# Where the expert matmuls stand in a block's window: ahead of or behind the next projection

## The reference

```python
x = layernorm(x + attn(x))         # conv (3 taps, 1024 -> 768), 16 heads in blocks of 128,
                                   # then o @ proj_w + proj_b, (256 -> 1024)
base = x @ W_base.T + b_base       # 1024 -> 1024
gate = softmax(x @ W_gate.T)       # 8 experts
thr = sigmoid(x @ W_thr.T + b_thr) / 8
w = max(gate - thr, 0); w = w / (sum(w) or 1)
h = x @ A.T                        # 8 experts of rank 16 -> 128 columns
moe = (h * w) @ B * 2              # 128 -> 1024
x = layernorm(x + base + moe)
```

## Time and profile before

| | us |
|---|---|
| median of 3 runs | 1800.07 (1799.27 to 1800.44) |
| the profiled execution's own time | 1800.44 |
| its span | 1798.6 |
| of the span, PE busy | 1743.6 (97%) |
| DVE busy | 1438.9 (80%) |
| ACT busy | 723.2 (40%) |
| POOL busy | 333.0 (19%) |

### The profile page before, as it was taken

One profiled execution on the slowest core, in us unless ns is written; L12 is line 12 of the kernel. 1 busy time (PEld: TensorE's weight loads), 2 busy tenths in 40 slices (PEclk: granted clock), 3 DMA queues, 4 the chain that ended last, 5 costly groups with the idle time before them and its releaser, 6 DMA issues. The chain is left out here.

```text
span 1798.6 us, 32713 instructions
## 1 busy us (share of the span) xinstructions
PE 1743.6 (97%) x11712; PEld 1599.5 (89%) x11712; DVE 1438.9 (80%) x3281; ACT 723.2 (40%) x1881; POOL 333.0 (19%) x276
## 2 busy tenths in 40 slices
PE   5899999999999799999999999999999999999998
PEld 5899999899999688888888888878898989898987
DVE  8977679977767688888888888887878787878785
ACT  4332334333324576767777767771111111111110
POOL 6100003400000110100101001134333333333331
PEclk9999999999999899999999999999999999999999
DMA  4323223432342101010110101223121212121211
GB/s 139 114 76 99 82 76 110 149 88 82 94 169 88 54 1 48 1 47 0 47 47 0 47 0 63 85 82 105 54 79 53 77 54 77 54 75 56 75 42 48
DMA packets 48804, 123.03 MB, mean 68 GB/s; under 512 B 5488, under 2 KB 13680, under 8 KB 48240
## 3 DMA queue, kind: packets, MB, share of 16 engines
q1 hardware_dynamic: 48752, 122.36, 20.6%
HBM read 88.79 MB, written 33.55 MB: 68 GB/s over the span
## 5 line engine op out<-in xcount | busy, mean ns | idle before, releaser
L388 PE MATMUL conv_acc<-x_split,weights 128*128 128x256 f32 x4608 | 555.2, 283 | 32.3 <-DVE weights L314 25.0
L388 PEld LDWEIGHTS conv_acc<-x_split,weights 128*128 128x128 f32 x4608 | 552.4, 190 | 34.9 <-DVE weights L314 26.5
L1343 PE MATMUL ps_f<-weights 128*128 128x266 f32 (+2 forms) x1728 | 329.0, 343 | 0.0
L1343 PEld LDWEIGHTS ps_f<-weights 128*128 128x128 f32 x1728 | 277.4, 189 | 23.5
L247 ACT ACTIVATE x_split<-x_mixed 128x1024 fp32r<-128x1024 f32 x128 | 135.7, 1060 | 305.7 <-PE conv_acc L388 276.7
L309 DVE TENSOR_TENSOR x_split<-x_mixed,x_split 128x1024 fp32r<-128x1024 f32 x128 | 158.3, 1237 | 99.9 <-ACT x_split L247 99.9
L720 ACT ACTIVATE scores_and_probs<-scores_and_probs,score_neg_max 128x128 f32<-128x128 f32 x512 | 197.9, 392 | 3.5 <-DVE score_neg_max L831 3.5
L1179 ACT ACTIVATE gate_exp<-h_and_gate,gate_neg_max 128x8 f32<-128x8 f32 x32 | 9.6, 301 | 347.1 <-DVE gate_neg_max L1254 347.1
L683 POOL TENSOR_TENSOR weights<-conv_tile,weights 128x1024 fp32r<-128x1024 f32 x14 | 36.1, 2576 | 476.0 <-ACT weights L703 384.6
L826 DVE CUSTOM_DVE_ANT_0 scores_and_probs<-ps_scores,causal_mask 128x128 f32<-128x128 f32 x512 | 117.8, 286 | 0.5
L1343 PE MATMUL ps_f<-q_k_pairs,weights 128*128 128x266 f32 (+2 forms) x576 | 117.0, 338 | 0.0
(11 more groups left out here) (118 smaller groups left out, 2651.7 us busy)
## 6 DMA issues: line engine op xcount, KB each, us to landing
x_raw<-in_xT SPq DMA_DIRECT2D x128, 257.0 KB, 2.7
conv_tile<-in_x SPq DMA_DIRECT2D x32, 512.0 KB, 3.4
out<-out_tile SPq DMA_DIRECT2D x32, 512.0 KB, 2.6
convT_scratch<-features_out SPq DMA_DIRECT2D x16, 768.0 KB, 3.5
conv_tile<-convT_scratch SPq DMA_DIRECT2D x16, 768.0 KB, 6.4
conv_w_raw<-in_conv_w SPq DMA_DIRECT2D x16, 576.0 KB, 3.9
weight_stage<-in_ffn_w SPq DMA_DIRECT2D x8, 581.0 KB, 3.7
yT_scratch<-features_out SPq DMA_DIRECT2D x8, 512.0 KB, 3.7
```

Source lines behind the costliest of these rows:

```text
L388: last = nc.tensor.matmul(acc[f][k // 2][:, k % 2, :], w[:, c, a, k, f * P:(f + 1) * P], xs[:, c % XS, b, k, :], start=(c == 0 and k % 2 = ...
L1343: mm = nc.tensor.matmul(ps_f[par][n][:, 0:b0 - a0], x1T[:, par, a, kc, :], wf[kc][:, b, a0:b0], start=(kc == 0 and k == 0), stop=(n == 2 a ...
```

## The change

In PE's window the call of `experts(i, par)` moves ahead of the call of `project(i + 2, par)`. No instruction is added, removed or changed.

```diff
                 base(i, par, 1, range(CC // 2, CC))
+                experts(i, par)
                 if not last(n, 2):
                     project(i + 2, par)
-                experts(i, par)
```

## The result

| kernel | median, us | range, us | runs |
|---|---|---|---|
| before | 1800.26 | 1799.27 to 1801.06 | 4 |
| after | 1813.99 | 1813.25 to 1815.96 | 4 |

The change makes the kernel slower: 13.7 us lie between the two medians. Three more executions of the kernel after took 1815.11, 1816.99 and 1817.49 us. The ratio of the means over all seven is 1.0084 (95% interval 1.0069 to 1.0098), which is 15.1 us. The forecast was 1813.8 us. The profiled execution of the kernel after has a span of 1813.9 us, 15.3 more than before's.

What follows compares the result with a forecast made beforehand. PE was taken to bound the last phase, with DVE not far behind. Lateness of 8.15 us plus restarts of 5.5 us gave 13.7 us, so 1813.8 us was predicted, range 1809 to 1820 us.

Steps and rivals of the forecast that it cites:

- DVE's chain: DVE's work from its second add of the projection to the end of L1282, 13.87 us, following project wherever it is put.
- The sum: Last phase: lateness 8.15 us plus restarts 5.5 us make 13.7 us, between 9.9 and 19.2.
- Window in the loop: Windows 4 to 27: experts 1.50, project's start to second add 2.96, chain 13.87, together 18.33 us, plus 0.19 restart.
- from project's start to the second add: Piece of the closed loop from PE's project start to DVE's add of the projection's second half, 2.96 us.
- the slack of windows 2, 3 and 28: Operand slack in windows outside the loop, taken as 1.31 us without being read; range widened to 1809 to 1820.
- The restart: PE resuming after each wait at the experts: 0.06 us wake-up plus 0.13 us first weight load, 29 times, 5.5 us.
- The high end: Restart in which PE's sequencer also loses its lead: 0.38 us a window, 11.0 us in all.
- A: Rival: DVE's normalising step takes 0.81 instead of 2.80 us, chain 11.88 us, PE never waits, 1800.1 us; 8%.
- B: Rival: restart costs far more than 0.38 us a window; at 0.6 us, 1825.6 us; 5%.
- C: Rival: short waits bring down PE's clock in the last phase, 1839 us; 4%.
- D: Rival: faster, because the experts' early end frees `ps_f` or smooths PE's order; 3%.

Runs made afterwards that it cites:

- e7: Kernel after with one 0.2 us instruction (L1268) left out of DVE's chain; median 1810.50 us, ratio to before 1.0043.
- e4: Kernel after with one more DVE instruction in the chain, L1246's split of y repeated into a spare tile; median 1826.83 us, ratio to before 1.0142.
- e5: Kernel before with one more DVE instruction, L1246's split of y repeated into a spare tile; median 1803.43 us, ratio to before 1.0011.
- e1: Kernel after with DVE's split_hT(i) put ahead of its split_xT(i + 1) in each window; median 1800.60 us, ratio to before 0.9993.
- e6: Kernel after with POOL's bias add (L1143) made on one column instead of 1024, from block 2 on; median 1800.38 us, ratio to before 0.9993.
- e8: Kernel before with six more DVE instructions in each window, L1246's split repeated into spare tiles; median 1829.91 us, ratio to before 1.0155.

## Why the prediction was right

*The spare time of the moved operand is not what the trace of before shows at its place.* The prediction read 1.20 us of slack and set 1.50 us of delay against it, because DVE's chain hangs on project. The trace after has the chain unchanged at 13.87 us and the wait where it was said, in 29 windows. e7 and e4 show that the chain enters the window one for one, e5 that it doesn't before.

*The sum.* Window in the loop: forecast 18.33 + 0.19 = 18.52, measured 18.51 in the turn shown above and up to 18.55 in others. From the first window to the last 14.3 us came on top, forecast 13.7. The excess is small and spread, 29 windows by 0.02 us. The piece that was too short is the one from project's start to the second add: forecast 2.96, measured 2.98 in 11 windows and 3.01 or 3.02 in 19. The 2.98 belong to the new order, for e1 has them without any wait (its second add starts at 1507.92, project at 1504.94). The rest shows in e4 and e7 too, where the experts wait for DVE, and not in e1 and e6, where they don't; what makes it was not looked for. That the medians lie 13.7 us apart, to the digit of the forecast, is luck: over all seven executions it is 15.1 us, and the time ahead of the phase varies by 1 us and more. The range was widened for the slack of windows 2, 3 and 28. That wasn't needed: their slots, too, open 1.3 us after the operand is ready.

*The restart.* The wake-up is 0.06 us as forecast; the experts' group is 1.77 us long behind the wait and 1.67 without, so the first load costs 0.10 where I took 0.13 from a group in the attention. Together 0.16 instead of 0.19, 0.9 us less over 29 windows, which hides a part of the excess above. The high end, in which the sequencer's lead is lost, did not show: after the wait project starts 1.60 us behind the experts, 1.50 + 0.10.

*The rivals.* A did not happen: POOL stayed 0.14 us ahead of DVE, the distance that hangs on POOL alone. Its chain of 11.88 us was 0.3 us too short, by e6; the time that it gives doesn't change by that. By the Trainium skill's rule (SBUF — State Buffer, "Who interferes with whom") the first to issue holds the shared ports and the other one blocks. That the two instructions disturb each other agrees with e6, where the short POOL instruction leaves DVE's at 0.81 us; that the order decides was not tested, for no run has it the other way round. The rule says that the second one blocks fully; here DVE's step of 0.81 us ends 0.55 us after POOL's, so by estimate 0.26 us of it ran beside POOL's. B did not happen, see the restart. C did not: the granted clock was 1.00 from 1222 to 1790 us. D, a gain from the order itself, shows in the traces but is tiny. Where the new order runs without waits, in e1 and e6, the first and last start of L1282 are closer together than before. Of e1:

```profile
L1282 DVE TENSOR_TENSOR h_weighted_T<-ps_f,h_weighted_T x32: 236/238/293, 1232.1 to 1786.0; 128x128 fp32r<-128x128 f32 x32
```

That is 553.9 us against 554.9, 0.03 us a window. Which border of PE's groups gives it was not tried apart, and the timed runs of e1 and e6 can't tell it from no change. So e1 is no version that beats the kernel before.

## What to carry to other kernels

This is one kernel, so take it as a question to ask and not as a law. Before moving a group of instructions ahead of another, ask what the one pushed back feeds: if it starts the chain whose end the moved group waits for, the slack in the profile shrinks by the whole length of the moved group (here 1.20 us less 1.50). Then compare the closed path (group, pushed-back group, chain) with the bound engine's own window; if it is longer, even by 0.3 us, it is paid in every turn, and a restart with it. Idle time on an engine says nothing about whether it is free to take more work as long as that idle time lies in a wait of such a path.

## What the runs showed of the hardware

- A DVE step of 0.81 us takes 2.79 us when a POOL instruction of 2.39 us has started 0.14 us before it; it ends about 0.55 us after POOL's. One POOL bias add thus costs this step 2.0 us a window; leaving it out in e6 shortened DVE's chain by 1.7 us.
- A wait on PE's weight load costs, over the wait itself, 0.06 us from DVE's end to PE's start and 0.10 us in the group of nine matmuls behind it (1.77 us against 1.67). The projection behind that group takes 2.78 us to the next group's start (1513.92 to 1516.70), as in e1 without a wait (1504.94 to 1507.72), and in 19 of 30 windows about 0.035 us more.
- In e8, PE waits 2.7 us for the gate in window 0 (its weight loads 3.0 us, above), where before has no such wait, and the granted clock of the next stretches is below 1.00:

```profile
1236.00:1240.00 4.00, 3.28 (x13) 3.29 (x13) 1.99 (x6) 0.58 (x2) 0.00 (x0) 0.67 0.00 0
1240.00:1244.00 4.00, 4.00 (x17) 3.31 (x17) 1.18 (x2) 0.00 (x0) 0.00 (x0) 0.90 0.00 0
```

  By estimate that is (1 - 0.67) x 4 + (1 - 0.90) x 4 = 1.7 us lost, once; means below 1.00 say that a part of each stretch ran at 1.2 GHz. In e5, where PE waits 0.73 us in the same place, the clock stays at 1.00 from 1222 to 1250 us; in the changed kernel, with weight loads that wait up to 0.6 us in 29 windows, it stays at 1.00 too.
